# High and low parts of a tail's feature blocks, made two neighbouring PSUM banks at a time

## What is computed

```python
def _mingru(x, Wz, bz, Wh, bh):
    z = sigmoid(einsum('bsi,hi->bsh', x, Wz) + bz)
    h_tilde = tanh(einsum('bsi,hi->bsh', x, Wh) + bh)
    a = clip(1.0 - z, 1e-08, 1.0 - 1e-08)
    return _linear_scan(a, z * h_tilde)          # along the 512 tokens

def _stack(x, Wz, bz, Wh, bh, gamma, beta):
    h = x
    for i in range(4):
        h_new = _mingru(h, Wz[i], bz[i], Wh[i], bh[i])
        if i > 0:
            h_new = h_new + h
        h = _layernorm(h_new, gamma, beta)       # over the 512 features
    return h

# _xcond: concatenate(_stack(x), flip(_stack(flip(x)))) @ fusion_W.T + fusion_b
x = x + _xcond(_layernorm(x), ...)
x = x + _ffn(_layernorm(x), ...)                 # gelu, layernorm, ternary weights
```

## Time and profile before

| | us |
|---|---|
| median of 3 runs | 1540.54 |
| lowest and highest | 1540.24, 1540.54 |
| the profiled execution, its own time | 1540.21 |
| its span, first to last instruction | 1538.4 |

### The profile page before, as it was taken

How to read it: one execution, slowest core, us unless ns; L and a number is a source line. 1 busy time by engine, 2 the same in 40 slices (tenths; PEclk the granted TensorE clock), 3 DMA queues, 4 the chain that set the end, 5 groups by cost and what they waited for, 6 DMA issues and landing times.

```text
span 1538.4 us, 22933 instructions
## 1 busy us (share of the span) xinstructions
PE 1518.7 (99%) x7744; PEld 1202.7 (78%) x7744; DVE 1307.8 (85%) x2021; ACT 1021.6 (66%) x1688; POOL 829.6 (54%) x1013
## 2 busy tenths in 40 slices
PE   9999999999999999999999999999999999999999
PEld 7877888888888888888888877777777777777776
DVE  8998999999899989999888887786877777776786
ACT  7988789898687897787987444445454444444354
POOL 6766657578868678676788632331423333332331
PEclk9999999999999999999999999999999999999999
DMA  4211212321312112122044551030302020111000
GB/s 171 76 37 68 103 56 90 124 69 63 123 40 85 56 41 90 65 94 89 29 145 143 193 171 42 1 110 1 96 15 89 22 89 22 62 48 41 29 20 36
DMA packets 73157, 113.20 MB, mean 74 GB/s; under 512 B 5193, under 2 KB 37961, under 8 KB 69970
## 3 DMA queue, kind: packets, MB, share of 16 engines
q1 hardware_dynamic: 72754, 111.21, 21.3%
q10 hardware_dynamic: 288, 0.52, 0.1%
HBM read 73.95 MB, written 37.77 MB: 73 GB/s over the span
## 4 chain that ended last, share of the span: by engine, by line
PE 50%; DVE 2%; ACT 1%; issue 0%; POOL 0%; DVEq 0%; ACTq 0%; POOLq 0%
PE ps L639 15%; PE ps L620 14%; PE ps L572 11%; PE ps L499 6%; PE ps L519 1%; PE ps L585 1%; PE ps L533 1%; PE ps L649 1%; DVE bnp L1132 1%; PE ps L662 0%; ACT H L876 0%; DVE H L1120 0%; DVE yb L1112 0%; ACT AH L880 0%; DVE H L1121 0%
## 5 line engine op out<-in xcount | busy, mean ns | idle before, releaser
L499 PE MATMUL ps<-AH,WH 128*128 128x512 f32 x896 | 366.9, 409 | 7.8 <-DVE H L1121 6.1
L499 PE MATMUL ps<-AL,WH 128*128 128x512 f32 x896 | 351.0, 392 | 0.0
L499 PE MATMUL ps<-AH,WL 128*128 128x512 f32 x896 | 349.4, 390 | 0.0
L1587 POOL TENSOR_TENSOR H<-H,yb 128x512 f32<-128x512 f32 x192 | 245.9, 1291 | 8.5 <-DVE yb L1112 1.3
L1112 DVE TENSOR_TENSOR_SCAN yb<-ab,ps 128x512 f32<-128x512 f32 x192 | 231.9, 1208 | 15.5 <-POOL ab L1578 9.1
L950 ACT ACTIVATE g<-ps 128x512 f32<-128x512 f32 x128 | 76.5, 598 | 248.7 <-PE ps L620 248.7
L837 ACT ACTIVATE yb<-ps,ncnd 128x512 f32<-128x512 f32 x224 | 158.2, 706 | 87.3 <-PE ps L499 84.2
L499 PEld LDWEIGHTS ps<-AH,WH 128*128 128x128 f32 x896 | 168.5, 188 | 46.3 <-DVE H L1121 8.6
L1307 DVE SCALAR_TENSOR_TENSOR gl<-g,wbcol,gh 128x512 fp32r<-128x512 f32 x118 | 116.9, 991 | 97.7 <-ACT gh L960 97.6
L499 PEld LDWEIGHTS ps<-AL,WH 128*128 128x128 f32 x896 | 168.1, 188 | 37.1
L1688 POOL TENSOR_TENSOR rs<-mv,nhalf 128x1 f32<-128x1 f32 x32 | 43.0, 1342 | 282.2 <-DVE mv L1279 282.2
(11 more groups left out here) (193 smaller groups left out, 3230.4 us busy)
## 6 DMA issues: line engine op xcount, KB each, us to landing
hs_scratch<-H SPq DMA_DIRECT2D x16, 1024.0 KB, 5.4
hc<-hs_scratch SPq DMA_DIRECT2D x32, 512.0 KB, 4.4
xr<-in_x SPq DMA_DIRECT2D x32, 256.0 KB, 4.5
out<-ob SPq DMA_DIRECT2D x32, 256.0 KB, 2.2
xbuf<-in_x SPq DMA_DIRECT2D x7, 1024.0 KB, 7.6
RAW<-in_wt SPq DMA_DIRECT2D x16, 256.0 KB, 6.3
stg<-in_fct SPq DMA_DIRECT2D x16, 256.0 KB, 3.2
stg<-in_pjt SPq DMA_DIRECT2D x16, 256.0 KB, 2.9
```

What stands on the lines that cost most here:

```text
L499: r = e.matmul(GATE[i % 3][:], w[:, q, m * 128:(m + 1) * 128], a[:, q, :], start=(n == 0), stop=(n == 11))
L1587: e.tensor_tensor(H[s][:, m, :], H[s][:, m, :], yb[i % 5][:], ALU.add).then_inc(s_v, 1)
```

## The change

For the forward tails of layers 0 to 2 ("f", 76 pairs of blocks in the slots), the feature blocks are now handled in the order 0, 1 and then 2, 3 instead of 2, 0, 1 and then 3: on PE (`back`), in the ring, on ACT and on DVE. ACT makes H of both blocks of a pair first and then one AH over two neighbouring PSUM banks (128x1024), and DVE makes one AL over the two (128x1024). Where the first block of a pair lies in bank 7, whose successor in the ring is bank 3, both stay single; that is so for 16 of the 76 pairs, so 60 are joined. PSUM becomes one tensor of eight banks so that two of them can be addressed together. On DVE, the low part of block 2 moves from ahead of scan block 1 to behind the low parts of blocks 0 and 1, and that of block 3 moves from behind stats pair 0 to ahead of it. Blocks of inputs ("x") and of backward layer-0 tails ("b") stay as they were.

```diff
-RING_SLOT = [("B", "x", -2, 2), ("B", "b", 3, 2), ("B", "f", 2, 2), ("B", "f", 2, 0), ("B", "f", 2, 1),
-    ("B", "x", -1, 0), ("B", "b", 3, 3), ("B", "f", 2, 3), ("B", "b", 3, 1), ("B", "x", -1, 1), ("B", "b", 3, 0),
+RING_SLOT = [("B", "x", -2, 2), ("B", "b", 3, 2), ("B", "f", 2, 0), ("B", "f", 2, 1),
+    ("B", "x", -1, 0), ("B", "b", 3, 3), ("B", "f", 2, 2), ("B", "f", 2, 3), ("B", "b", 3, 1), ("B", "x", -1, 1), ("B", "b", 3, 0),
...
-    PS = [ctx.enter_context(nc.psum_tensor(f"ps{i}", [128, 512], F32)) for i in range(8)]
+    ps = ctx.enter_context(nc.psum_tensor("ps", [128, 8, 512], F32))
+    PS = [ps[:, i, :] for i in range(8)]
...
+    def two_banks(n):
+
+        return ps[:, RING_PS[n % 5]:RING_PS[n % 5] + 2, :]
...
             mm(job(s), 1)
-            back("h", tail(s - 2), 2)
             back("h", tail(s - 2), 0)
             back("h", tail(s - 2), 1)
             back("x", batch(s + 1), 0)
             back("h", tail_b(s - 3), 3)
+            back("h", tail(s - 2), 2)
             back("h", tail(s - 2), 3)
...
+        def feature_pair(idx, p):
...
+            n, s = BANK[("h", idx, 2 * p)], place(TAILS[idx])
+            for m in (2 * p, 2 * p + 1):
+                e.wait_ge(s_t2, T2N[("h", idx, m)] + 1)
+                e.activation(H[s][:, m, :], RING[BANK[("h", idx, m)] % 5][:], ACT.Identity, bias=bet[:, m:m + 1],
+                             scale=gam[:, m:m + 1]).then_inc(s_h, 1)
+            if RING_PS[n % 5] < 7:
+                e.activation(AH[s][:, 2 * p:2 * p + 2, :], two_banks(n), ACT.Copy).then_inc(s_ah, 2)
+                return
...
-            feature("h", tail(s - 4), 2)
-            feature("h", tail(s - 4), 0)
-            feature("h", tail(s - 4), 1)
+            feature_pair(tail(s - 4), 0)
             feature("x", batch(s - 1), 3)
             feature("h", tail_b(s - 5), 3)
-            feature("h", tail(s - 4), 3)
+            feature_pair(tail(s - 4), 1)
...
+        def low_pair(idx, p):
...
+            e.wait_ge(s_ah, HIGHS[("h", idx, 2 * p + 1)])
+            e.tensor_tensor(AL[s][:, m, :], two_banks(n), AH[s][:, m, :].bitcast(F32), ALU.subtract).then_inc(s_al, 2)
...
         for s in SLOTS:
-            low("h", tail(s - 4), 2)
             low("x", batch(s), 2)
             low("x", batch(s - 1), 3)
             scan(job(s - 2), 1)
             low("x", batch(s - 1), 0)
-            low("h", tail(s - 4), 0)
-            low("h", tail(s - 4), 1)
+            low_pair(tail(s - 4), 0)
             low("h", tail_b(s - 5), 3)
+            low_pair(tail(s - 4), 1)
             stats(tail(s - 3), 0)
             low("h", tail_b(s - 5), 1)
-            low("h", tail(s - 4), 3)
```

## The result

The changed kernel takes 1574.49 us (median of 4 runs, 1573.75 to 1575.79) against 1540.54 us before: 34 us more, ratio 1.0222 (95% interval 1.0204 to 1.0239). The direction was as forecast, the size twice the forecast 16.4 us, and the time lies outside the range of 1544 to 1566. Two of the four executions ran at a mean granted clock of 1.000 (1573.75 and 1573.98) and two at 0.999 (1575.00 and 1575.79); the last of these is the one profiled.

The account below looks back on a forecast made before the run. PE bounds the kernel (busy 1518.7 of 1538.4 us), so only its waits count: 9.1 + 5.8 + 3.5 = 18.4 us new, less 2, gives 16.4 and 1557.0 us (1540.21 + 16.4, median 0.33 higher); range 1544 to 1566.

Parts of the forecast that it names:

- stats pair 0: On DVE behind both double low parts: 1.55 us late in a quiet slot, priced at 5.8 + 3.5 us of PE waits.
- the busy slot of the earlier trace: Near 457 us, DVE's queue reaches 458.79 and PE waits 1.6 us for the second token bank.
- the 5.8: PE's feature transposes behind norm pair 1 wait for late stats in eleven slots: 5.8 us in all.
- the 3.5: Tokens pair 1 wait for banks that norm pair 0 leaves, in three slots behind a layer-0 job: 3.5 us.
- ACT's room: ACT's idle time between norm pairs 0 and 1, absorbing late stats: 1.23 us in a quiet slot, 0.56 in early ones.
- these six cost nothing: Six late second-token-bank slots ahead of the long layer-0 scan waits (8.6 us): PE arrives later and finds the scan done.
- The 15 late slots: Of 38 forward-tail slots, 15 get the second token bank over 0.3 us late, by up to 1.7 us.
- only the first pair's banks were priced: Token-bank waits were counted only for the second bank of tokens pair 0, behind blocks 0 and 1: 9.1 us.
- the deductions for the slot before: In nine late slots, delay already caused by the slot before was taken off, leaving 9.1 us of second-token-bank waits.
- rival 3: In the stack, nothing is absorbed and every first-order delay counts: about 27 us more, 1567 us; 13 in 100.
- Rival 1: On DVE, fewer instructions and a moved low part remove six scan waits of 8.6 us: 1532 us; 7 in 100.
- rival 2: In the stack, new token waits are paid back by later scan waits, no change: 1540 to 1543 us; 10 in 100.

Follow-up runs that it names:

- j1: Kernel before with blocks 0 and 1 joined at the old places, except in slots around a backward layer-0 tail (19 joins): 1540.81 us, ratio 1.0001.
- j2: Against e7, only the low part of block 3 moved ahead of stats pair 0, all single: 1550.76 us, ratio 1.0065.
- h1: Kernel before with ten transposes repeated ahead of the second token bank in six slots followed by long layer-0 scan waits: 1544.92 us, ratio 1.0028.
- e7: Changed kernel with all instructions single and DVE's low parts at their old places: 1540.33 us, ratio 1.0000.
- i2: Changed kernel with only the second pair (blocks 2 and 3) joined, the first pair single: 1570.30 us, ratio 1.0193.
- f2: Changed kernel with only the low parts on DVE joined, high parts on ACT single: 1577.31 us, ratio 1.0235.
- e8: Against e7, the low part of block 0 also moved behind the scan, all single: 1551.33 us, ratio 1.0068.
- f1: Changed kernel with only the high parts on ACT joined, low parts on DVE single: 1566.60 us, ratio 1.0168.
- i1: Changed kernel with only the first pair (blocks 0 and 1) joined, the second pair single: 1566.71 us, ratio 1.0171.
- e5: Changed kernel with the first joined low part moved ahead of the scan of block 1 on DVE: 1571.40 us, ratio 1.0197.
- e1: Against e8, the low part of block 3 moved ahead of stats pair 0, all single: 1558.20 us, ratio 1.0116.
- e1b: Against e1, ACT's order changed from H, AH, H, AH to H, H, AH, AH, all single: 1561.27 us, ratio 1.0134.

## Why the prediction was wrong in size

**Right.** That PE's work does not change and the rest of the program is untouched; that the saving on DVE and ACT is worth nothing (j1); the durations, 1060 and 1216 ns against the 1060 and 1200 taken; and that stats pair 0 behind all low parts is expensive. In the slot that was worked out, H starts at 365.14 now and norm pair 0 at 373.79, 8.65 later against 7.00 before: 1.65 late where 1.55 was forecast, and ACT's idle time before gates block 0 is gone:

```profile
365.14 1.45 ACT L895 ACTIVATE H<-ps,bet,gam 128x512 f32<-128x512 f32 x2
366.47 1.04 ACT L898 ACTIVATE AH<-ps 128x1024 fp32r<-128x1024 f32 x1
...
373.79 1.45 ACT L855 ACTIVATE ntok<-ps,nbp,rsp 128x512 f32<-128x512 f32 x2 [2.36 <-POOL nbp L1632]
...
376.27 0.70 ACT L843 ACTIVATE yb<-ps,ncnd 128x512 f32<-128x512 f32 x1
```

Right too was the busy slot of the earlier trace rows: PE was to wait 1.6 us for the second bank, and waits 1.6 by start times, of which the profile shows 1.47:

```profile
475.87 0.60 PE L525 MATMUL ps<-ident,H 128*128 128x128 f32 x4
477.93 0.66 PE L525 MATMUL ps<-ident,H 128*128 128x128 f32 x4 [1.47 <-DVE AL L1175]
```

**Right in the sum, by luck in its parts: stats pair 0.** It was priced at 5.8 + 3.5 = 9.3 us and measured alone at 10.1 (j2). But in the trace of j2 the 5.8 for the feature transposes behind norm pair 1 are 2.4 (from 6.1 to 8.5 by start times), and the 3.5 for the tokens that want the bank of norm pair 0, in three slots, are 7.7, in nine. Where ACT's room was to be used up, less was lost than I counted; where a bank had little room, three times as many slots paid.

**Wrong, first: "these six cost nothing".** The 15 late slots had a raw lateness of 17.4 us in my working; measured are 17.7, of which 0.9 stood there before. I took 5.1 of it off as paid back by the six waits for a scan, because DVE works without a gap there. It did, but only as long as PE was on time: stats pair 1 stood 0.36 us behind PE's first bank of tokens. Measured, PE waits 5.7 us in these six slots, and the six waits for the scan behind them shrink by 2.1 only (from 7.1 to 5.0 by start times). h1 shows the same by itself: 0.72 of 1.09 us are left over. All waits for scans shrank by 3.4 us, not by 5.1 and the further small waits.

**Wrong, second: only the first pair's banks were priced.** The claims of tokens on the banks of blocks 2 and 3 stand in the same ring. In e7 half of them are free 1.8 us or more in time, and I gave the forward tail's second bank alone a price; but the nine that now wait had 0.14 us or less, in the kernel before as in e7. In the changed kernel these claims cost 9.8 us against 1.0, and joining this pair alone costs 9.0 (i2). It is the largest term that was missing.

**Wrong, third: the deductions for the slot before.** From the nine other late slots I took off 3.2 us, because PE would already be late, and was left with 9.1. Measured in the nine are 12.0, of which 0.9 stood there before: for example 1.64 instead of 0.92 near 400 us, 1.63 instead of 1.35 near 478, 1.52 instead of 1.20 near 254. My reading is that DVE was behind by work of the same slot, and that its late stats moved it back as much as PE; no run tests this alone.

**Not counted, and small: the clock.** The prediction took it as full throughout. In the profiled execution 1.6 us are lost to a lower clock, behind the longest of the new waits.

So rival 3, nothing is absorbed, was the nearest in kind and still 7.5 us short, since it lacked the second pair. Rival 1 and rival 2 have fallen.

Two single low parts take 1344 ns by their durations and a joined one 1216, 128 less; from start to start it is 1.18 us against 1.12 (two joined ones, from 476.68 to 478.92), 0.06 less. The Trainium skill gives a price of 125 ns for an instruction of DVE that reads PSUM (Perfetto Trace Analysis, Optimizing Scalar/DVE Operations). The durations here agree with it, the starts do not. As it says itself, grouping can help where the engine is saturated; here the joined low part on DVE made the kernel 16.0 us slower (f2).

Sum of the steps as measured: old places 0, first low part behind the scan +11.0, block 3 ahead of stats +6.9, grouped on ACT +3.1, joins +13.2: 34.2 us (at full clock 10.3, 7.6, 2.5 and 13.2). No version tried is faster than the kernel before. Not tried was AH ahead of both H on ACT: DVE would then read a bank while ACT still reads it for H.

## What to carry to other kernels

Before joining instructions over buffers that go round in a ring, list for every buffer who asks for it next and by how much it is free in time: a joined instruction frees the first buffer only with the last, and all the claims in the ring count, not only the first, and each place by itself: here half the claims had 1.8 us to spare and the nine that cost most had 0.14 at best. Where the engine that would get faster is not the one that ends last, as here, the saving is worth nothing, and every slack of a few tenths that the join uses up becomes a wait. And do not book a new wait against an old one behind it, unless the engine you then wait for needs nothing from the one that is late now.

## What the hardware showed beyond that

A wait costs PE a little more than itself. Four transposes of a token bank take 0.60 us when they follow at once and 0.66 when they follow a wait, in the pairs of rows at 352 and 476 us above. Summed over the stack, the start times of transposes that wait for nothing moved by 2.2 us between the two kernels with the same instructions. Why a sequence restarts more slowly was not tested.

Matmuls that wait for nothing moved by 1.8 us, and 1.6 of it stand in one place, behind the longest new wait. The profiled execution, PE, and then the window of 131 to 132 us (its clock is the third figure from the end):

```profile
126.99 0.63 PE L525 MATMUL ps<-ident,H 128*128 128x128 f32 x4 [0.20 <-DVE xbuf L1254]
129.98 0.73 PE L525 MATMUL ps<-ident,H 128*128 128x128 f32 x4 [2.36 <-DVE AL L1175]
130.94 0.63 PE L505 MATMUL ps<-AH,WL 128*128 128x512 f32 x1
131.37 0.63 PE L505 MATMUL ps<-AL,WH 128*128 128x512 f32 x1
131.00:132.00 1.00, 1.00 (x4) 0.81 (x3) 1.00 (x3) 0.00 (x0) 0.00 (x0) 0.50 0.52 174
```

PE is busy for 0.64 of the 3 us from 127 to 130. Then the granted clock is 0.50, the lower of its two levels (1.2 GHz), for 3.4 us, and the next matmul starts after 0.43 us instead of 0.23. The traces of e8, f1 and i1 have the same 3.4 us at this place, e5 has them twice elsewhere, and the other traces not at all. The wait alone does not decide it: PE idles 2.36 us here in the changed kernel, in i1 and in f2, and f2's traced execution keeps the full clock; it idles 1.8 us here in e1, e1b, i2, e8 and f1, and only the last two lose the clock. Executions of one kernel differ in it: e8 takes 1550.42 and 1550.75 us at a mean clock of 1.000, and 1551.90 and 1552.24 at 0.999. What tips it was not tested.
